# Decoder layer on one core: where the fourth expert group, the routing, the last two batches and the prologue's loads and scatters stand in the order of work

## The reference

```
x  = x + local_attention(layernorm(x)) @ w_out        # 16 heads of 8, causal, blocks of 64 with the block before
x  = x + cross_attention(layernorm(x), ctx)           # K and V weights chosen per row of ctx by its bucket (8), masked by times
y0 = layernorm(x)
y1 = LN1(y0 + mha(y0))                                # 4 heads of 32, over the batch axis
gates = softmax(y1 @ wg); idx = argmax(gates)         # 8 experts
keep  = place of the row within its expert < 256      # capacity, counted over all rows in order
moe   = keep * gate[idx] * ((y1 @ w1[idx] + b1[idx]) @ w2[idx] + b2[idx])
out   = LN2(y1 + moe)
```

## Time and profile before

| | us |
|---|---|
| median of 3 runs | 355.65 (354.18 to 358.45) |
| the profiled execution, its own time | 355.05 |
| its span, first to last instruction | 353.2 |
| mean granted TensorE clock | 0.966 of full |

### The profile page before, as it was taken

The page is one execution under the profiler, slowest core; times in us unless marked ns, Lnnn a source line. Parts: engine busy times, 40 slices in busy tenths (PEclk is TensorE's granted clock), DMA queues, the critical chain, the costliest instruction groups (busy, mean ns, idle before and its releaser), DMA issues.

```text
span 353.2 us, 12288 instructions
## 1 busy us (share of the span) xinstructions
PE 319.6 (90%) x4774; PEld 219.2 (62%) x4774; DVE 264.7 (75%) x675; ACT 163.0 (46%) x443; POOL 119.9 (34%) x193
## 2 busy tenths in 40 slices
PE   7659998999999999999999999888788789899991
PEld 3325574666666565656565565565566478799991
DVE  5856789667777999999999989444454459769994
ACT  2124465655566555555656464533145472203331
POOL 1074534000000555553243523245100013105996
PEclk9896999999999999999999999999999999589997
DMA  8850412354582265995920000000000000306112
GB/s 232 258 154 29 148 51 77 115 150 149 173 210 95 75 140 150 203 245 156 221 66 3 2 2 4 5 0 2 2 2 4 2 2 1 108 32 225 31 32 59
DMA packets 36697, 31.89 MB, mean 90 GB/s; under 512 B 4792, under 2 KB 33600, under 8 KB 36512
## 3 DMA queue, kind: packets, MB, share of 16 engines
q1 hardware_dynamic: 34080, 27.37, 27.3%
q0 software_dynamic: 1280, 3.15, 3.5%
q10 hardware_dynamic: 1280, 0.59, 0.6%
HBM read 23.40 MB, written 7.70 MB: 88 GB/s over the span
## 4 chain that ended last, share of the span: by engine, by line
PE 65%; DVE 10%; POOL 9%; DMA 6%; issue 4%; ACT 3%; SPq 1%; POOLq 0%; DVEq 0%
PE ps L1185 9%; PE ps L1239 9%; PE ps L1222 8%; DMA ctx_sorted<-room 3%; PE ps L1159 3%; PE ps L1195 3%; PE ps L1138 3%; PE ps L1272 3%; PE ps L1308 3%; PE ps L1151 3%; POOL rs L868 3%; DMA room<-ctx_sorted 2%; POOL room L873 2%; POOL y L875 2%; PE ps L1322 2%
## 5 line engine op out<-in xcount | busy, mean ns | idle before, releaser
L912 ACT ACTIVATE pT<-ps 128x512 f32<-128x512 f32 x128 | 73.7, 609 | 79.4 <-PE ps L1195 77.1
L803 POOL TENSOR_TENSOR rstd<-veps,minus_half 128x1 f32<-128x1 f32 x32 | 19.2, 599 | 112.1 <-DVE veps L432 112.1
L467 DVE TENSOR_REDUCE m_pad<-ps 128x8 f32<-128x1024 f32 x32 | 39.0, 1220 | 16.0 <-PE ps L1222 16.0
L443 DVE TENSOR_TENSOR p_sb<-qk_sb,heads 128x512 f32<-128x512 f32 x64 | 44.0, 687 | 0.7 <-DMA ident_bf<-c_ident_bf 0.3
L470 DVE TENSOR_REDUCE m_pad<-ps 128x8 f32<-128x1024 f32 x32 | 38.9, 1215 | 0.0
L1222 PE MATMUL ps<-p_sb,qk_sb 32*128 32x512 f32 x256 | 38.4, 671 | 0.0
L868 POOL TENSOR_TENSOR rs<-ve,half 128x2 f32<-128x2 f32 x16 | 14.2, 890 | 67.7 <-DVE ve L685 67.6
L1185 PE MATMUL ps<-p_sb,qk_sb 32*128 32x512 f32 x256 | 37.2, 651 | 0.0
L1574 PE MATMUL ps<-mexp,pT 128*128 128x128 f32 x256 | 33.6, 287 | 1.4 <-DVE room L785 1.2
L1239 PE MATMUL ps<-pT,p_sb 128*32 128x128 f32 x1024 | 34.6, 276 | 0.0
L1574 PEld LDWEIGHTS ps<-mexp,pT 128*128 128x128 f32 x256 | 31.5, 201 | 2.1 <-DVE pT L759 1.1
(11 more groups left out here) (192 smaller groups left out, 653.5 us busy)
## 6 DMA issues: line engine op xcount, KB each, us to landing
room<-mask_rows SPq DMA_DIRECT2D x32, 128.0 KB, 3.7
wkv_sb<-wkv SPq DMA_DIRECT2D x23, 128.0 KB, 2.1
kv_sorted<-room SPq DMA_DIRECT2D x5, 512.0 KB, 3.2
w1t_sb<-w1t SPq DMA_DIRECT2D x8, 256.0 KB
w_sb<-w SPq DMA_DIRECT2D x8, 256.0 KB
kv_sb<-hot_rows SPq DMA_DIRECT2D x4, 512.0 KB, 4.4
ctx_sorted<-room SPq DMA_DIRECT2D x1, 1472.0 KB, 11.6
tk<-fside SPq DMA_DIRECT2D x1, 1024.0 KB
```

Source lines behind the costliest of these rows:

```text
L443: return dve.tensor_tensor(dst, rows.unsqueeze(1).broadcast_to([128, QUADS, S]), heads[:, 0, :].unsqueeze(2).broadcast_to([128, QUADS, S]) ...
L467: dve.tensor_reduce(m4[:, 0:2, 0:QUADS], ps[:, 0:2, :].rearrange("p g (j k) -> p g j k", j=QUADS), AX.X, ALU.max).then_inc(s["max_low"], 1)
L912: act.activation(pT[:, t % 2, g, :, :], quad[4 + g], ACT.Exp).then_inc(s["exped"], 1)
```

## The change

1. `heads` is loaded second and has a semaphore of its own, `heads_in`; DVE waits for that alone. SP waits for all constants to land before it issues ctx and the zeros; the loads of x (batches 4 to 15) and `w_out` come behind them.
2. `bucket_slots` is split: `bucket_tiles` (the first six steps) stands before the maxima of tile 0, the other seven stand behind `keys_by_head(1)` and the statistics of tile 3. POOL does the power of tile 3 ahead of any scatter, and scatters 4, 3, 3, 2, 2, 2 over periods -1 to 4. On TensorE `count_buckets` goes ahead of `project_qkv(1)` in place of two idle products, and `turn_xn(2)` behind `scores_by_query(0)`.
3. Expert group 0 moves from period 31 to 30, and group 3 from period 36 to step 16 of the first norm's loop. It waits there until bank 0 is free.
4. `same_position(0)` of the first group stands ahead of `mha_project(3, ...)`; `mha_weighted` waits for each exponential in turn.
5. `place(0)` goes ahead of `ffn(0)`; `route_picks(1)` behind the step of gated(3), `route_gates(1)` behind that of gated(5), `turn_picks(1)` and `place(1)` behind `ffn(3)` and `ffn(4)`.
6. Batches 12 and 13 are finished on DVE instead of ACT and POOL, and batches 14 and 15 one at a time with a power each (`last_power`); ACT stores 14 and 15 singly.

```diff
-EXPERT_PERIODS = (T - 1, T + 1, T + 3, T + 4)
+EXPERT_PERIODS = (T - 2, T + 1, T + 3)
+SCATTERS = (range(0, 4), range(4, 7), range(7, 10), range(10, 12), range(12, 14), range(14, 16))
...
-            sp.dma_start(x_sb[:, 4:B, :], ...)
-            sp.dma_start(w_out_sb[:, 0, :], w_out)
+            sp.wait_ge(s["heads_in"], 16)
+            sp.wait_ge(s["sort_in"], 48)
+            sp.wait_ge(s["consts_in"], 32)
             sp.dma_start(ctx_sb[:, :, :], ...)
             sp.wait_ge(s["zeros_ready"], 1)
             sp.dma_start(ctx_sorted..., zeros...)
+            sp.dma_start(x_sb[:, 4:B, :], ...)
+            sp.dma_start(w_out_sb[:, 0, :], w_out)
...
                 if p == -1:
-                    keys_by_head(1)
-                    bucket_slots()
+                    bucket_tiles()
                 if live(p + 1):
                     maxima(p + 1)
...
                 if live(p + 1):
                     queries_by_head(p + 1)
+                if p == -1:
+                    keys_by_head(1)
+                    norm_stats(3)
+                    norm_aggregate(3)
+                    norm_variance(3)
+                    bucket_slots()
...
                 if p == -1:
-                    norm_stats(3)
-                    norm_aggregate(3)
-                    norm_variance(3)
                     norm_rows(3)
...
-                if p == -1:
-                    for b in range(4):
-                        scatter_ctx(b)
                 if live(p + 4):
                     norm_power(p + 4)
                 if -1 <= p < 5:
-                    for b in range(2 * p + 6, 2 * p + 8):
+                    for b in SCATTERS[p + 1]:
                         scatter_ctx(b)
...
                 if m == 1:
-                    route_picks(1)
                     route_gates(0)
-                if m == 4:
-                    route_gates(1)
...
-                    if b % 2:
+                    if b % 2 and b < B - 2:
                         pair_variance(b, 1)
+                    if b == B - 3:
+                        for a in (b - 1, b):
+                            z_scaled(a, 1, ln_rows[:, 2, :])
+                    if b == B - 2:
+                        last_variance(b)
+                        z_scaled(b, 1, ln_rows[:, 2, :])
+                        for a in (b - 2, b - 1):
+                            z_rows(a, 1, x_sb[:, a, :], y0, "last_rows")
+                if m == 3:
+                    route_picks(1)
+                if m == 5:
+                    route_gates(1)
+            z_rows(B - 2, 1, x_sb[:, B - 2, :], y0, "last_rows")
+            last_variance(B - 1)
+            z_scaled(B - 1, 1, ln_rows[:, 2, :])
+            z_rows(B - 1, 1, x_sb[:, B - 1, :], y0, "last_rows")
...
-                pe.wait_ge(s["f_exped"], 4 * i + 4)
                 for j in range(MH):
+                    pe.wait_ge(s["f_exped"], 4 * i + max(j, 1) + 1)
...
             for m in range(B + 6):
                 project_and_turn(m)
+                if m == 16:
+                    experts(3)
...
                 if m == 20:
+                    place(0)
                     ffn(0)
-            place(0)
             for b in range(1, B):
                 if b + 1 < QUADS:
                     spread_hot(b + 1)
                 ffn(b)
-                if b == 1:
+                if b == 3:
                     turn_picks(1)
-                if b == 2:
+                if b == 4:
                     place(1)
```

More of the change, by code:

```diff
@@ L880, in _, with last_power @@
                 pair_power(i, 0)
-            for i in range(B // 2):
+            def last_power(b):
+                pool.wait_ge(s["ve_ready"], B + B // 2 + b - (B // 2 - 1) + 1)
+                pool.tensor_tensor(rs16[:, b:b + 1], ve16[:, b:b + 1], half16[:, 0:1], ALU.pow).then_inc(s["rs_ready"], 1)
+            for i in range(B // 2 - 1):
                 pair_power(i, 1)
@@ L1096, in _ @@
             gate_exps(1)
-            for i in range(B // 2 - 1):
+            for i in range(B // 2 - 2):
                 for b in (2 * i, 2 * i + 1):
```

76 lines of the change are left out of this document (46 added, 30 removed).

## The result

The kernel after takes 343.48 us (median of 6 runs, 342.39 to 343.83), the kernel before 355.46 (354.00 to 358.45), a ratio of 0.9654 with a 95% interval of 0.9611 to 0.9696. The forecast was 345.9 with a range of 342.5 to 350.5. The profiled execution took 343.83 of its own, with a span of 342.0. Against the earlier trace rows the page has TensorE busy for 3.4 us less, VectorE busy as long as before, and a clock that falls only at the start.

The account below looks back on a forecast made before the run. TensorE, busy 90% of the span, bounds the kernel; gains lie where it works less or stands still. Terms 4.0 + 0.1 + 2.25 + 0 + 1.25 + 1.3 + 0.9 = 9.8 from 355.05 give 345.25, plus 0.6: 345.9, range 342.5 to 350.5.

Parts of the forecast that it names:

- Prologue, 4.0: Prologue: a walk along VectorE's list puts tile 1's maxima at 18.8, 4.5 us earlier; taken as 4.0 for late hand-overs.
- rival (b): Prologue: the clock no longer falls at 26, 3.0 us more is won, 342.9; chance 0.12.
- (c): Sorted rows, period 6: bunched scatters make TensorE wait, giving back the prologue's 4.0 us, 349.9; chance 0.11.
- (d): Statistics of tile 4: x rows of tiles 4 to 15 land too late, past 35.4 us, kernel slower; chance 0.03.
- Group 3, 2.25: Period 36: expert group 3 leaves the path, winning its 1.88 us and 0.35 idle before it, 2.25 in all.
- Group 0, 0.1: Periods 30 and 31: moving expert group 0 wins 0.1 us, between -0.4 and 0.5.
- Second attention, 1.25: Second attention: splitting the wait lets three of four denominators run beside the exponentials; 1.25 us over the groups, 0.8 to 1.8.
- Picks' wait and gated products, 1.3: Picks' wait: the fourth group fills TensorE's hole, the clock stays up, and `ffn(6)` starts 1.3 us earlier.
- rival (a): Picks' wait: the clock falls all the same, the term becomes -1.0 us, 348.2; chance 0.30 together with (e).
- Rival (e): Gated products: the routing's move does nothing because `ffn` waits for VectorE, 1.3 us less, 347.2; chance 0.30 with (a).
- The end, 0.9: End: VectorE finishes rows 12 to 15 and a one-batch store follows; wins 0.9 us, bounds -0.5 and 1.3.
- the marks that I had named: Trace signs per place, such as maxima of tile 1 at about 19 and the Ln about 0.7 earlier in all groups.

Follow-up runs that it names:

- the fillers: Kernel after with three more idle products behind the projection of tile 2 and three behind the first turn of the maxima: 350.85 us, ratio 0.9757.
- the undone version: Kernel after with one wait for all four exponentials ahead of the denominators, as before: 350.29 us, ratio 0.9769.
- the last experiment: Kernel after with expert loads spread and each group's last exponential of the second attention cut into two halves, a denominator product for each: 341.59 us, ratio 0.9607.
- the control: The kernel after, unchanged, run again: 343.09 us, ratio 0.9681 to the kernel before.
- the first four experiments: Kernel after with prologue undone (ratio 0.9806), TensorE's hole at 14 to 16 filled (0.9757), group 3 back in period 36 (0.9840), one wait for the exponentials (0.9769).

## Why the prediction was right, and where it was not

The whole was right: faster, inside the range, 2.4 us below the number named (0.7%). It was right by a sum in which three terms were too small and one was too large. That it came so close is in part luck: against the profiles' 11.2, 4.1 were missing in the terms (2.1 in the prologue, 1.4 in the gated products, 0.4 at the end, 0.15 in group 3), and 2.65 were lost on the other side (1.15 in the second attention, 1.25 at tile 20 and 0.25 ahead of it).

1. *Prologue, 4.0.* The walk along VectorE's list held to 0.4: second maxima 18.8 in the forecast, 19.06 and 18.5 to 19.2 in the profiles. What failed is the step from there to the sum: the 4.5 of the walk were cut to 4.0, and nothing was set for what TensorE's clock gives behind it. At the maxima of tile 8, 4.3 to 6.4 are won against the kernel before's 71.07. The excess over the walk is rival (b), half come true: the clock is at 1.00 from 26 to 32, but falls once earlier, between 14 and 26. That the new prologue's stretch of idle is shorter, as (b) argued, fits with it; it is not shown that this is the reason, for the fillers moved nothing that can be told from chance. The loads' share, 0.9 in the walk, was 0.6 at the first keys between the first two profiles (9.09 and 8.46) and about 2 with the loads undone. Rivals (c) and (d) fell: x is not waited for, and TensorE waits for the sorted rows in period 6 as before (0.55 for 0.53), but 6.1 earlier. I had named a wait there as a sign of being wrong; by itself it is not one, for the kernel before had it too.
2. *Group 3, 2.25.* Measured 2.4, and undone 2.4. Group 0, 0.1: measured 0.1 with `same_position`.
3. *Second attention, 1.25.* This is the step that failed outright: "of 1.07 0.27 stays behind the last one". It gave 0.1. The four denominators write four groups of 32 partitions and run side by side; each is two passes of 512 columns. In the first profile one pass alone takes 0.59 and seven together 1.41; eight behind one another in the list took 1.06 in the undone version. The last one costs after the last exponential what all four did. The Trainium skill (TensorE: Matmul & The Clock Gate, Part 3, Measured speedup vs the span model) says that a pack of such products takes one product's duration and about 4 ns for each further tile. The rows agree, and that rule would have given 0 for this term. What shortens it is fewer columns in the last product, which the last experiment shows with 0.28.
4. *Picks' wait and gated products, 1.3.* The mechanism, that the hole stands ahead of the clock's fall and the group fills it, is shown by three runs: with the group 69.4, without it 71.6 and a clock of 0.57, with 1.0 us of idle products in its place 69.1 and a clock of 1.00. In all eleven profiles with the group there the clock is 1.00 behind it, so rival (a) fell. The size was off in two steps. `gated(0)` was not to come earlier, and `ffn(0)` at 307.4; it starts at 299.47, with the 7.1 won before it 306.6, because the group's excess was 0.3 and not 0.9. And from `ffn(0)` to `ffn(6)` I had 16.3, where 15.7 passed: the waits for VectorE, 0.91 and 0.50, are about what I set down (1.5), but the two spreads took 0.9 and not 1.2, and the turn and the places 0.6 and not 1.0. Rival (e) was true in its statement and wrong in its price: the routing's order is worth 0.1, not 1.3.
5. *The end, 0.9.* 6.32 us passed from the start of `ffn(15)` to the last compute instruction's end in the kernel before, 5.38 in the kernel after: 0.9, as worked out. Another 0.4 lies behind it (353.2 - 350.31 against 342.0 - 339.48), where a store of one batch stands in place of one of two. I had set nothing for it; that the smaller store is the reason is not shown. By the rule of the Trainium skill (GPSIMD Engine Reference, section 8, Key points) the power of batch 14 would be long. The trace does not agree in this place: it took 0.59 beside VectorE's row instructions, as long as the power of batch 15, in both profiles of the kernel after. The kernel before's rows had shown it already: the power that took 0.73, at 347.64, also lay beside two of VectorE's row instructions (347.27 to 348.09), and the one of 1.66 beside its 128x1024 products.

Of the marks that I had named all came but the Ln, which is 0.05 earlier and not 0.7. What I had not priced was the 1.25 at tile 20; it is in some executions and not in others of the same list of instructions.

## What to carry to other kernels

A hole in TensorE's list can cost more than its length if the clock falls behind it (here 2.5 us, behind waits of 1.04 and 0.58): put work from the path into it, and measure the stretch behind the hole, not the hole. It does not hold for every hole: the fill at 14 to 16 gave nothing that could be told. Before a wait is split, ask what the last product costs by itself; where products run side by side, as here, splitting their wait gave 0.05 us a group and cutting the last one's columns 0.28. And where one kernel's profiles differ by 1 to 3 us from one execution to the next, read an edit between two marks that hold in all of them, not in the total.

## What was not expected of the hardware

TensorE stood still in the middle of its list, with no wait that the profile shows, where the DMA engines were full (a share of 0.98 to 1.14 from 146 to 156): 1.12, 0.50, 0.94, 1.87, 1.67, 1.67 and 0.58 us in seven profiles, in five of them ahead of the same 13 mask products, and not at all in the control, which has the same list and a share of 1.02. With the kernel before (1.00) and the one with only the loads undone (1.13) none came either, so full DMA engines are not enough. Behind the stands of 1.67 and 1.87 the clock was below 1.00 in the windows of 2 us that follow (0.51 to 0.64), so they cost twice. On the chip of the first four experiments smaller ones, 0.3 to 0.4, came at a DMA share near 0.5 in tiles 1 to 4 of the new prologue. That instructions come late because they are brought by the same DMA engines would fit, for the list of DMA queues has two of kind instruction with packets in these windows, and the place is so often the same; but the control has such packets there as well. No run here isolates it, and this stays open.
